# A fused hybrid block on one core: jobs of the shared PSUM bank, attention blocks and softplus steps put at other units of the loop

## What is computed

```python
xn = (x - mu) * rsqrt(var + 1e-05) * ln_g + ln_b          # x is already layer-normed once
delta = softplus(dt_in @ w_dt + b_dt);  A = -exp(A_log)   # dt_in, Bs, Cs from xn @ w_xproj
h = exp(dt[:, :, None] * A) * h + (dt * xt)[:, :, None] * bt[:, None, :]   # scan over 512 tokens
ssm_out = (einsum('bdn,bn->bd', h, ct) + x * D_ssm) @ w_ssm_out
scores = einsum('bhnqd,bhnkd->bhnqk', qb, k3) / sqrt(HD)  # 16 blocks of 32 queries, 96 keys each
ao = einsum('bhnqk,bhnkd->bhnqd', softmax(scores + bias), v3)
conv_out = silu(depthwise_conv4(x) + b_conv)
eo = softmax(x @ dec.T / sqrt(D)) @ dec                   # 512 memory slots
x + 0.2*attn_out + 0.45*ssm_out + 0.15*conv_out + 0.2*(x @ w_wm + b_wm + 0.3*eo)
```

## Time and profile before

| what | value |
|---|---|
| runs | 1168.51, 1164.86, 1168.54 us; median 1168.51 us |
| the profiled execution | 1166.9 us, span 1165.1 us, mean granted TensorE clock 0.83 |
| busy in the span | DVE 988.3 us (85%), POOL 951.5 us (82%), PE 866.0 us (74%), ACT 835.1 us (72%) |
| first scan to last | starts at 37.7 us, ends at 1141.0 us, then 24.1 us of tail |

### The profile page before, as it was taken

How to read it: one execution, slowest core, us unless ns; L and a number is a source line. 1 busy time by engine, 2 the same in 40 slices (tenths; PEclk the granted TensorE clock), 3 DMA queues, 4 the chain that set the end, 5 groups by cost and what they waited for, 6 DMA issues and landing times. The chain is left out here.

```text
span 1165.1 us, 19124 instructions
## 1 busy us (share of the span) xinstructions
PE 866.0 (74%) x4151; PEld 361.1 (31%) x4151; DVE 988.3 (85%) x2306; ACT 835.1 (72%) x2247; POOL 951.5 (82%) x668
## 2 busy tenths in 40 slices
PE   4477769687786787777786777867768687778775
PEld 2132323232333233333232333323233233333332
DVE  2699998888897997979989799788998989898992
ACT  4668786877778776777777777587776876766671
POOL 6479997988888887888979898698887988788892
PEclk8558998778897977979889788787989788897797
DMA  5845766565756566566656476555666566656640
GB/s 121 202 127 147 199 164 171 133 169 163 181 153 159 156 158 165 146 155 167 165 166 165 118 192 169 141 147 148 173 167 177 137 166 169 174 157 173 159 113 9
DMA packets 124397, 181.18 MB, mean 156 GB/s; under 512 B 29266, under 2 KB 41062, under 8 KB 124262
## 3 DMA queue, kind: packets, MB, share of 16 engines
q1 hardware_dynamic: 123974, 179.56, 58.9%
q10 hardware_dynamic: 288, 0.20, 0.1%
HBM read 170.79 MB, written 5.05 MB: 151 GB/s over the span
## 5 line engine op out<-in xcount | busy, mean ns | idle before, releaser
L1391 POOL TENSOR_TENSOR prod<-hst,C 128x1024 f32<-128x1024 f32 x256 | 601.7, 2353 | 156.7 <-DVE hst L1201 155.9
L1201 DVE TENSOR_TENSOR_SCAN hst<-decay,bank 128x512 f32<-128x512 f32 x384 | 459.5, 1206 | 16.0 <-POOL prod L1391 15.1
L659 ACT ACTIVATE decay<-wide,A_rep 128x512 f32<-128x512 f32 x384 | 273.9, 715 | 72.8 <-DVE hst L1201 55.0
L1189 DVE TENSOR_TENSOR bank<-bank,B 128x512 f32<-128x512 f32 x384 | 261.7, 681 | 48.8 <-PE bank L938 23.0
L905 PE MATMUL bank<-spread,sel_bc 96*128 96x512 bf16 x384 | 170.0, 444 | 145.3 <-DVE hst L1201 137.0
L673 ACT ACTIVATE prob<-s_sb,nmax 128x96 f32<-128x96 f32 x512 | 184.8, 363 | 1.5 <-DVE nmax L1214 0.5
L1407 POOL TENSOR_TENSOR uwide<-uwide,B 128x512 f32<-128x512 f32 x128 | 162.7, 1271 | 21.8 <-DMA uwide<-u_rows 21.8
L929 PE MATMUL bank<-prod,sel_red 128*32 128x512 f32 x1024 | 171.7, 750 | 2.0 <-POOL prod L1391 2.0
L1201 DVE TENSOR_TENSOR_SCAN hst<-bank,uwide 128x512 f32<-128x512 f32 x128 | 155.0, 1211 | 6.1 <-ACT bank L659 4.6
L938 PE MATMUL bank<-k,q 128*128 128x384 f32 x256 | 133.6, 609 | 7.3 <-DVE nmax L1214 4.8
L945 PE MATMUL bank<-ident,prob 128*96 128x128 f32 x512 | 99.4, 328 | 48.9 <-ACT ao L689 44.2
(11 more groups left out here) (188 smaller groups left out, 1014.6 us busy)
## 6 DMA issues: line engine op xcount, KB each, us to landing
wide<-dt_rows SPq DMA_DIRECT2D x512, 256.0 KB, 4.6
uwide<-u_rows SPq DMA_DIRECT2D x128, 256.0 KB, 4.1
spread<-parts SPq DMA_DIRECT2D x66, 32.0 KB, 3.4
x_sb<-in_L_attn_x_dram SPq DMA_DIRECT2D x8, 256.0 KB, 4.1
dt_rows<-sp_t SPq DMA_DIRECT2D x8, 256.0 KB, 3.9
out_dram<-outb SPq DMA_DIRECT2D x8, 256.0 KB, 2.3
vw<-v_tok SPq DMA_DIRECT2D x80, 16.0 KB, 3.3
u_rows<-uv SPq DMA_DIRECT2D x8, 64.0 KB, 3.6
```

What stands on the lines that cost most here:

```text
L659: nc.scalar.activation(to, wide[m % SLOTS][:, s % 2, :], ACT.Exp, scale=A_rep[:, g:g + 1]).then_inc(exp_done, 1)
L1189: v.tensor_tensor(uP[s % 4][:, :], uP[s % 4][:, :], B2[p][:, :], ALU.mult).then_inc(dbx_done, 1)
L1201: v.tensor_tensor_scan(hst[:, s % 4, :], kept, into[:, :], 0.0, ALU.mult, ALU.add).then_inc(scan_done, 1)
L1391: g.tensor_tensor(prod[:, 2 * (m % 4):2 * (m % 4) + 2, :], hst[:, 2 * (m % 2):2 * (m % 2) + 2, :], C2[p][:, :].unsqueeze(1).to_broadcast([ ...
```

## The change

1. Attention blocks start every three units from unit 6 (6, 9, ..., 51) and no longer at 33k/10 (0, 3, 6, 9, 13, ..., 49).
2. The value job `v` moves from unit 62 to unit 21 of the batch before, ahead of `B`, `C`, `q` and `k`; `q` and `k` move from 58 and 60 to 60 and 62. SP's 12 DMAs that spread the values go from pairs 0 to 3 to pairs 4 to 6, after the batch's first scores.
3. Softplus: DVE's `softplus_rounding` is gone. ACT subtracts 1 (one more `Copy`, unit 20) and POOL subtracts e (`lost`, unit 22); `log1p`, `dt`, `u` follow at 23, 24, 25.
4. `output` goes from 27 to 29, `zT` from 22 to 23; the convolution's taps are two per unit in 39 and 40, tanh at 40, gate at 42; the memory jobs move by one to three units.
5. In batch 7 eight parts of `project` go into units 60 to 63, two in each, where before there were six, one in each of 58 to 63.

```diff
-JOB_AT = {13: ("t", "back"), 15: ("p", "xaT"), 17: ("p", "xnT"), 19: ("p", "dtpre"),
-          22: ("t", "zT"), 26: ("t", "ffn"), 28: ("m", "es0"), 32: ("p", "B"), 33: ("p", "C"), 34: ("m", "pt0"),
-          39: ("m", "conv"), 42: ("m", "es1"), 46: ("m", "es2"), 50: ("m", "pt1"), 51: ("m", "es3"),
-          55: ("m", "pt2"), 57: ("m", "pt3"), 58: ("p", "q"), 60: ("p", "k"), 62: ("p", "v")}
+JOB_AT = {13: ("t", "back"), 15: ("p", "xaT"), 17: ("p", "xnT"), 19: ("p", "dtpre"), 21: ("p", "v"),
+          23: ("t", "zT"), 26: ("t", "ffn"), 30: ("m", "es0"), 34: ("p", "B"), 35: ("p", "C"), 37: ("m", "pt0"),
+          40: ("m", "conv"), 43: ("m", "es1"), 47: ("m", "es2"), 51: ("m", "pt1"), 53: ("m", "es3"),
+          57: ("m", "pt2"), 59: ("m", "pt3"), 60: ("p", "q"), 62: ("p", "k")}
...
+LAST_PROJECT = {60: (0, 1), 61: (2, 3), 62: (4, 5), 63: (6, 7)}
...
-    "softplus_logs": 21, "rounding": 23, "log1p": 24, "dt": 25, "u": 27, "high": 30, "r": 32,
+    "softplus_logs": 21, "lost": 22, "log1p": 23, "dt": 24, "u": 25, "high": 28, "r": 30,
...
-SCORES_AT = {33 * k // 10: k for k in range(NBLK)}
+SCORES_AT = {6 + 3 * k: k for k in range(NBLK)}
...
         def softplus_step(eng, B, name):
-            steps = {"log1p": (sp_l, sp_l, sp_t, ALU.subtract),
+            steps = {"lost": (sp_t, sp_t, sp_e, ALU.subtract),
+                     "log1p": (sp_l, sp_l, sp_t, ALU.subtract),
...
             def window_values(B, which):
 
                 wait(sp, done["p"], job_count("p", B, "v"))
+                if first(B):
+                    sp.wait_ge(const_ready, 3)
+                else:
+                    wait(sp, s_ready, B * NBLK + 1)
...
                 nc.scalar.activation(sp_t[:, :], sp_e[:, :], ACT.Identity, bias=1.0).then_inc(sp_step, 1)
+                wait(act, sp_step, B * N_SP + SP["sum"])
+                nc.scalar.activation(sp_t[:, :], sp_t[:, :], ACT.Copy, bias=-1.0).then_inc(sp_step, 1)
...
-                    tap = s - JOB_SLOT["conv"] + TAPS - 1
-                    if 0 <= tap < TAPS:
-                        conv_tap(B, p, tap)
+                    for tap in range(TAPS):
+                        if s == JOB_SLOT["conv"] - 1 + tap // 2:
+                            conv_tap(B, p, tap)
...
-            def softplus_rounding(B):
-
-                dve.wait_ge(sp_step, B * N_SP + SP["ln"])
-                v.scalar_tensor_tensor(sp_t[:, :], sp_t[:, :], 1.0, sp_e[:, :], ALU.subtract, ALU.subtract) \
-                    .then_inc(sp_step, 1)
...
-                        for name in ("log1p", "dt", "u"):
+                        for name in ("lost", "log1p", "dt", "u"):
                             if s == AT[name]:
                                 softplus_step(g, B + 1, name)
```

More of the change, by code:

```diff
@@ L56 @@
     "reduce": 3, "y_copy": 5, "project": 1, "proj_copy": 12, "residual": 14, "aggr2": 16, "root2": 17,
-    "normalise2": 20, "ffn": 25, "output": 27,
+    "normalise2": 20, "ffn": 25, "output": 29,
     "ln_stats": 0, "ln_aggr": 2, "ln_root": 4, "ln_apply": 11, "scale_xn": 12, "softplus_exp": 20,
-    "softplus_logs": 21, "rounding": 23, "log1p": 24, "dt": 25, "u": 27, "high": 30, "r": 32,
-    "mid": 35, "lo": 37,
-    "tanh": 39, "gate": 40,
+    "softplus_logs": 21, "lost": 22, "log1p": 23, "dt": 24, "u": 25, "high": 28, "r": 30,
+    "mid": 33, "lo": 35,
+    "tanh": 40, "gate": 42,
 }
 SETUP_AT = 5
-ROWS_AT = {"store": 14, "rows": 15}
-VALUE_DMA_AT = {0: (0, 1, 2), 1: (3, 4, 5), 2: (6, 7, 8), 3: (9, 10, 11)}
-PART_DMA_AT = {17: 0, 19: 1, 20: 2}
+ROWS_AT = {"store": 15, "rows": 14}
+VALUE_DMA_AT = {4: (0, 1, 2, 3, 4, 5), 5: (6, 7, 8), 6: (9, 10, 11)}
+PART_DMA_AT = {16: 0, 18: 1, 20: 2}
 M_MAX_LAG, M_EXP_LAG, M_INV_LAG, M_DIAG_LAG = 2, 3, 4, 5
-SCORES_AT = {33 * k // 10: k for k in range(NBLK)}
+SCORES_AT = {6 + 3 * k: k for k in range(NBLK)}
 BIAS_LAG, EXP_LAG, INV_LAG, NORM_LAG, PT_LAG, PT_COPY_LAG, PV_LAG, AO_COPY_LAG = 2, (3, 4), 6, 5, 9, 9, 11, 11
@@ L103 @@
 SP = {n: i + 1 for i, n in enumerate(
-    ["abs", "relu", "exp", "sum", "ln", "lost", "log1p", "dt", "u", "hi", "r", "mid", "lo"])}
+    ["abs", "relu", "exp", "sum", "less", "ln", "lost", "log1p", "dt", "u", "hi", "r", "mid", "lo"])}
 N_SP = len(SP)
@@ L1026, in body @@
             def body(B, p):
-                before[0] = ("p", B, "v")
+                before[0] = ("p", B, "k")
                 for s in range(UNITS):
@@ L1062, in body @@
                         mem_job(name, B, p)
-                    if last(B) and 0 < s - JOB_SLOT["pt3"] <= N_EARLY:
-                        project(B, p, s - JOB_SLOT["pt3"] - 1)
+                    if last(B):
+                        for n in LAST_PROJECT.get(s, ()):
+                            project(B, p, n)
             def tail(B, p):
-                for n in range(N_EARLY, N_PROJ - 1):
+                for n in range(8, N_PROJ - 1):
                     project(B, p, n)
```

10 lines of the change are left out of this document (3 added, 7 removed).

## The result

| | before | changed |
|---|---|---|
| median of 4 runs each, same chip | 1168.53 us (1164.86 to 1169.88) | 1122.49 us (1119.59 to 1127.89) |
| the profiled execution; its span | 1166.9; 1165.1 us | 1124.4; 1122.6 us |
| first scan; tail after the last scan | 37.7; 24.1 us | 38.9; 25.6 us |

The ratio of the runs is 0.9616, 95% interval 0.9571 to 0.9662: the medians differ by 46 us (39 to 50 by the interval). The forecast was 1131 us, in a range of 1090 to 1164; 1131 is 2 us above the upper end of the interval (1129).

A forecast was written before the change was run, and what follows sets the result against it. No engine fills the batch; DVE, near its floor, loses the rest standing at waits. Terms -32 + 0 - 10 + 3 + 1 + 2 = -36 us from 1166.9 gave 1131 us, range 1090 to 1164.

The forecast's parts named there:

- Part 1: Batch boundary: DVE's waits for scores and the issue wait go whole, 4.2 us of others too; -32 us, bounds 0 and -40.
- a sign of being wrong: The prediction called itself wrong if, among other signs, DVE waits for PE in units 1 to 11.
- rival D: Boundary: PE's clock stays low to unit 6, DVE waits 7.8 us in each of 7 boundaries; 1186 us, chance 0.11.
- Part 2: Softplus and last layer, units 19 to 29: removed waits return as waits for decay, bank, scores; 0 us, bounds -48 and +17.
- Part 3: Gate after the convolution: 1.0 us of wait left of about 2.3, in 8 batches; -10 us, bounds -18 and +8.
- Part 4: POOL: one subtraction more, DVE's waits for products stay and get a little longer; +3 us, bounds -7 and +14.
- Part 5: Ends: +1 us before the first unit (0 to +3), +2 us in batch 7 (-2 to +4).
- A: Units 24 to 29: waits go too, with PE's clock at 2.4 GHz; -21 us, 1110 us, chance 0.12.
- B: Units 21 to 25: POOL holds DVE back, 2.5 us more per batch in 7 batches; 1149 us, chance 0.13.
- C: Whole batch: waits move on, only 8 of 42 us from boundary and gate stay won; 1165 us, chance 0.09.

The follow-up runs named there:

- v_last: Changed kernel with the value job back last at unit 62, and q, k and the later memory jobs back too: 1169.15 us, ratio 1.0016.
- mem_old: Changed kernel with only the memory jobs pt1 and es3 back in units 50 and 51: 1149.81 us, ratio 0.9854.
- gate_40: Changed kernel with the convolution's gate back in unit 40, the unit of the tanh: 1150.29 us, ratio 0.985.
- root16: Changed kernel with POOL's small steps that normalise2 waits for in unit 16 and no longer in 17: 1110.97 us, ratio 0.9523.
- act_longer: Changed kernel with one more 0.63 us copy on ACT among the softplus steps, read by nobody: 1134.82 us, ratio 0.9744.
- corr_dve: Changed kernel with the softplus correction back on DVE in unit 23, without ACT's subtraction and POOL's lost: 1119.0 us, ratio 0.9597.
- scores_dma_old: Changed kernel with attention blocks at the old units and the values' DMAs back in pairs 0 to 2: 1157.13 us, ratio 0.9918.

## Why the prediction came out right

The forecast of 1131 us is 8.5 us above the median; against the profiled executions, by which its sum was made, it missed by 6.5 (-36 for -42.5). Direction and mechanism held: DVE no longer stands at the boundary's scores and at the gate, and the middle stays as it was. By its steps:

- **Part 1, the boundary: right in kind, too large.** -18.0 where it had -32. The wait for scores in unit 2 went. But the sum took the earlier trace rows's 23.0 us of scores as all of the boundary's (19.6 are, in units 2 and 5), and the places before show that the boundary stood only 32.6 us over the span, so -32 was all of it. The step that was mis-sized is "I take the first two (27.8) whole" with nothing put in their place: 14.6 us stay, nearly all DVE's waits for PE in units 0 to 8 while `project` runs, which the prediction had named as a sign of being wrong. That is rival D in small: passes at 1.9 us per two until the clock comes back, none of it in batches 1 and 2 and 1.6 to 4.5 us in the five others, not 7.8. The prediction counted against D that PE was back at the high level by unit 2. That is so in batch 4, which it had read; in batches 3 and 5 of the kernel before, the clock was at the low level for the first 7.0 and 7.8 us. It also put part of the gain down to the removal of `v`; v_last against mem_old shows 0.3 us for that. Undoing the scores' spacing gives back 7.3 us at the boundary. Undoing the memory jobs gives 3.9, but gate_40, whose edit is far from it, gives 3.8, so this is spread. What the other 10 us or so hang on no run told apart.
- **Part 2, the middle: right, by its chain.** Decay of unit 24 after 16.2 us predicted, 15.7 measured; wait for scores in unit 29 2 us predicted, 2.4 measured in batch 4 and 1.9 in the mean; sum 0 predicted, -3 measured. The wait for PE's bank of unit 28 did not come; there is one of 0.8 us for that of unit 24. Another name was wrong: not the scan waits for the decay but the reciprocal before it, for exponentials that stand behind the decay. What the sum had only as "a normalisation ahead of the small steps" is ACT's stand of 1.66 us ahead of `normalise2`; root16 shows what ending it, with the wait for POOL's product, is worth. act_longer and corr_dve bear the chain out.
- **Part 3, the gate: -14.0 for -10.** The 1.0 us of wait that were left in the count did not come; only 0.4 per batch behind the gate stay, and 1.2 once. gate_40 shows the distance to be what does it.
- **Part 4, POOL: wrong in sign.** -7.5 for +3 by place. The step that failed is "DVE's waits for products after the layer norm's small steps stay": before, two of POOL's normalisations stood among those small steps, of blocks with scores in units 0 and 3; with the first scores in unit 6 they do not exist at that place. scores_dma_old brings the wait for the product for scan 10 back (9.2 us over the span, as before). At the other such place the forecast held: the wait for the product for scan 22 grew from 2.8 to 9.5 us, for there a normalisation does now stand among the small steps. The table counts this with the middle; by the list of waits POOL's products went from 15.1 to 13.3, -1.8 for +3. I had asked what POOL gets in softplus, and not what leaves it elsewhere.
- **Units 44 to 60: -3.2, not in the sum.** This is within the spread. mem_old shows how sharp this place is: 27 us for two jobs moved by one and two units.
- **Part 5, the ends: +1.2 and +1.5 for +1 and +2.** Right.

Of the rivals, A (the middle's waits go too) came in a small part: the granted clock in the like stretch of batch 4 is 0.65, against 0.51 in the earlier trace rows, and DVE still waits, but in batch 1 it is 0.79 and the wait for scores 1.6 us shorter. The pair of mem_old's batches shows that A's price per batch was about right, 2.3 us for a clock at the high level where it had 3. B's term, POOL, was no bound; the 1.58 us wait for its product in unit 22 is its trace, and root16 took that away. C is excluded by the interval, and so is D as a whole. (The range's lower end is 4 us off its own terms: 1110 less half of 48 is 1086.) The errors of parts 1 and 4 have opposite signs (14 too much, 10.5 too little), with 4 us of the gate, 3 of units 44 to 60 and 3 of part 2 also on the side of too little. That the sum missed by 6.5 us and not 14 is in part luck. A batch came to 129.8 to 134.9 us in six of eight cases, 132.4 in the mean, where about 134 had been forecast; DVE's and POOL's work per batch, 120.4 and 118.6 us, is what had been forecast.
